# The cross-attention part of a perceiver block stepped by single groups, and eight wide products taken out of the delta-rule layers

## What is computed

```python
sa = attention(y, y, y, causal=True)
y = layernorm(y + sa, g1, beta1)
ca = attention(y, Z, Z, causal=False)      # Z: 257 rows of context for each sequence
y = layernorm(y + ca, g2, beta2)
h = jax.nn.relu(jnp.einsum('bsd,df->bsf', y, w1) + b1)     # DFF = 512
ff = jnp.einsum('bsf,fd->bsd', h, w2) + b2
y = layernorm(y + ff, g3, beta3)
```

## Time and profile before

| what | us |
|---|---|
| median of three runs | 762.5 |
| the profiled execution, whole time | 763.72 |
| its span, first to last instruction | 761.9 |
| first to last step of the cross part on VectorE | 8.6 to 111.7 |
| X in its new layout, VectorE goes on | 123.7 |
| the rest: two layers, routing, experts | 123.7 to 761.9 |
| mean granted TensorE clock | 0.853 |

### The profile page before, as it was taken

One profiled execution on the slowest core, in us unless ns is written; L12 is line 12 of the kernel. 1 busy time (PEld: TensorE's weight loads), 2 busy tenths in 40 slices (PEclk: granted clock), 3 DMA queues, 4 the chain that ended last, 5 costly groups with the idle time before them and its releaser, 6 DMA issues.

```text
span 761.9 us, 15678 instructions
## 1 busy us (share of the span) xinstructions
PE 625.3 (82%) x6640; PEld 427.1 (56%) x6640; DVE 461.8 (61%) x1124; ACT 256.4 (34%) x555; POOL 97.1 (13%) x140
## 2 busy tenths in 40 slices
PE   2777951786899999694997699978888799999995
PEld 1434641475688858464796678776444344444442
DVE  5846694978966354748828822475556855555552
ACT  1455510742421623642632034214323122222221
POOL 2535452300000001301100001010011000000000
PEclk9888985955599999897768658976899999999998
DMA  9994021000000000000000050000032163333321
GB/s 343 291 375 160 1 83 29 0 2 2 2 3 4 3 1 3 0 3 0 2 3 2 2 178 2 2 2 1 0 80 65 57 161 94 96 97 108 88 81 28
DMA packets 18981, 46.68 MB, mean 61 GB/s; under 512 B 3456, under 2 KB 8192, under 8 KB 18656
## 3 DMA queue, kind: packets, MB, share of 16 engines
q1 hardware_dynamic: 18368, 45.43, 19.3%
q10 hardware_dynamic: 544, 0.26, 0.1%
HBM read 43.32 MB, written 2.36 MB: 60 GB/s over the span
## 4 chain that ended last, share of the span: by engine, by line
PE 66%; DVE 22%; ACT 3%; DMA 3%; POOL 2%; issue 2%; SPq 1%; DVEq 0%; POOLq 0%
PE psum L753 7%; PE psum L748 7%; PE psum L758 7%; PE psum L685 5%; PE psum L594 5%; PE psum L560 3%; PE psum L711 3%; PE psum L714 3%; PE psum L674 3%; PE psum L621 3%; PE psum L667 2%; PE psum L720 2%; PE psum L571 2%; DVE yr L1287 2%; PE psum L464 2%; DVE pcT L1287 2%
## 5 line engine op out<-in xcount | busy, mean ns | idle before, releaser
L932 ACT ACTIVATE arena<-psum 128x512 f32<-128x512 f32 x68 | 40.6, 598 | 136.0 <-PE psum L748 122.9
L1363 DVE TENSOR_TENSOR arena<-psum,arena 128x512 f32<-128x512 f32 x64 | 44.2, 691 | 59.6 <-PE psum L753 57.8
L758 PE MATMUL psum<-arena,wed_sb 128*128 128x512 f32 x128 | 66.8, 604 | 0.0
L776 ACT ACTIVATE arena<-psum 128x512 f32<-128x512 f32 x56 | 33.3, 600 | 69.7 <-PE psum L560 41.0
L1368 DVE TENSOR_TENSOR arena<-arena 128x512 f32<-128x512 f32 x64 | 44.3, 692 | 14.0 <-PE psum L758 13.8
L560 PE MATMUL psum<-arena 32*64 32x128 f32 x1024 | 41.9, 327 | 6.6 <-ACT arena L776 2.8
L952 POOL TENSOR_TENSOR ve<-ss,eps_rms 128x4 f32<-128x4 f32 x16 | 3.7, 230 | 340.5 <-ACT yr L827 252.9
L560 PEld LDWEIGHTS psum<-arena 32*64 32x64 f32 x1024 | 36.8, 165 | 12.6 <-ACT arena L776 4.1
L753 PE MATMUL psum<-yT,weu_sb 128*128 128x512 f32 x68 | 36.3, 616 | 7.9 <-DVE arena L1363 7.9
L758 PEld LDWEIGHTS psum<-arena,wed_sb 128*128 128x128 f32 x128 | 24.6, 192 | 31.3 <-issue 22.7
L1314 DVE TENSOR_TENSOR arena<-psum,small 128x1024 f32<-128x1024 f32 x24 | 28.2, 1214 | 14.2 <-PE psum L667 14.2
(11 more groups left out here) (283 smaller groups left out, 1290.2 us busy)
## 6 DMA issues: line engine op xcount, KB each, us to landing
arena<-shares SPq DMA_DIRECT2D x64, 256.0 KB, 3.9
arena<-in_ctx_t SPq DMA_DIRECT2D x16, 514.0 KB, 8.9
arena<-in_ctx_z SPq DMA_DIRECT2D x16, 512.0 KB, 10.5
XA<-in_x SPq DMA_DIRECT2D x1, 1024.0 KB, 5.1
zlast<-in_ctx_last SPq DMA_DIRECT2D x4, 256.0 KB, 17.7
x_mid<-XA SPq DMA_DIRECT2D x4, 256.0 KB, 3.0
weg_sb<-in_we_gate SPq DMA_DIRECT2D x2, 512.0 KB, 6.5
weu_sb<-in_we_up SPq DMA_DIRECT2D x2, 512.0 KB, 7.5
```

The lines of the kernel that those rows point to most:

```text
L758: pe.matmul(x3, wed_sb[:, (p - 1) % (NPAIR + 1), :], act_a[pr], start=(p == 0), stop=False, skip_group_check=True).then_inc(x_down[pr], 1)
L776: return act.activation(out_, in_, ACT.Copy, scale=scale)
L932: act.activation(act_g[pr], banks[4 * pr + 2 * (n % 2)], ACT.Silu).then_inc(x_silu[pr], 1)
L1363: dve.tensor_tensor(act_gu[pr], banks[4 * pr + 1], act_g[pr], ALU.mult).then_inc(x_gu[pr], 1)
```

## The change

The cross part is no longer stepped by pairs but by single groups. Each group has a chain of its own up to its self attention (`BEFORE`) and one behind its cross attention (`AFTER`); the cross steps stay one chain for each pair. The letters a and b are `BEFORE` of the groups 0 and 1, c the cross steps of pair A, d and e `AFTER` of 0 and 1; v, w, x, y, z are the same for pair B. The transposes' removal from PSUM becomes a step of its own (`ev1`, `ev2`), and so does the last half of the last norm (`fin`, L1188). Counts for the waits come from a function instead of by hand; three semaphores are merged into others. A group's first transposes now land in its high bank, and the two banks of the feed-forward products are one low and one high bank of the group, so that `up` waits for the last use of the transposes' bank. GpSimd's bias for `XA` (L987) is one group at a time. SyncE's order of waits and copies stays. The engines' instructions are the same in number, but for the last hunk: the eight wide products in `lout` are removed.

```diff
-CROSS = ["st0", "nm0", "sas", "sap", "sar", "nm1", "c0", "c1", "c2", "c3", "c4", "c5", "cr0", "c6", "c7", "c8", "c9", "cr1",
-         "nm2", "up0", "up1", "dn", "nm3"]
-XTURNS = "AABAABABBABAAAAAABABABABAABABBAABBBABBBABABBBB"
+BEFORE = ["st0", "nm0", "sas", "sap", "sar", "nm1", "ev1"]
+AFTER = ["cr", "nm2", "ev2", "up", "dn", "nm3", "fin"]
+
+
+XTURNS = ("ababwvaavabvbaawbccvbvbcwcccwvvdcwxcxccdwwexdxxxydxdeyeyxdexxdzyezyyzyeezzzz")
...
+    chains = {}
+    for pr, (g0, g1, steps, h0, h1) in enumerate(("abcde", "vwxyz")):
+        for u, name in ((0, g0), (1, g1)):
+            chains[name] = iter([(kind, u, pr) for kind in BEFORE])
+        chains[steps] = iter([("c", n, pr) for n in range(NU * GT + 2)])
+        for u, name in ((0, h0), (1, h1)):
+            chains[name] = iter([(kind, u, pr) for kind in AFTER])
+    return [next(chains[turn]) for turn in XTURNS]
...
-                        pe.wait_ge(a_yT[pr], NU + (2 if n else 1))
+                        pe.wait_ge(a_yT[pr], count("yT", pr, "ev1", v))
...
+                low, high = banks[bank + u], banks[bank + 2 + u]
...
+                elif kind == "nm2":
+                    pe.wait_ge(a_norm[pr], count("norm", pr, kind, u))
+                    pe.wait_ge(at_exp[pr], count("exp", pr, "c", NT - NU + u))
+                    transposes(low, yn, g, a_tr[pr])
+                elif kind == "up":
                     pe.wait_ge(w_in, N_WEIGHT)
...
+                    if u == 0:
+                        pe.wait_ge(at_pT[pr], NT)
+                    for c in range(FFC):
+                        if c >= 2:
+                            pe.wait_ge(ff_h[pr], count("h", pr, kind, u) - FFC + c - 1)
+                        pe.matmul((high, low)[c % 2], w1_sb[:, c * P:(c + 1) * P], zT[g][:, :],
+                                  start=True, stop=True).then_inc(ff_up[pr], 1)
...
                     elif kind == "lout":
-                        if u == 0:
-                            dense(banks[bank + 2], 8)
                         pe.wait_ge(l_inv, pi + 1)
                         from_lanes(b1, pr, u).then_inc(l_omm[u], 1)
...
+                    if k == 2:
+                        pool.wait_ge(a_scaled[pr], count("scaled", pr, kind, u) - 2)
+                        pool.tensor_tensor(r[g], y[g], bc(rowv[:, B2:B2 + 1, :], [P, GT, D]),
+                                           ALU.add).then_inc(a_scaled[pr], 1)
+                        x_g = gcols(XA, g).rearrange("p (j c) -> p j c", j=GT)
+                        pool.wait_ge(a_vec[pr], count("var", pr, "nm0", u))
+                        pool.tensor_tensor(x_g, x_g, bc(rowv[:, BE3:BE3 + 1, :], [P, GT, D]),
+                                           ALU.add).then_inc(a_scaled[pr], 1)
...
+                elif kind == "fin":
+                    dve.wait_ge(a_rstd[pr], count("rstd", pr, "dn", u))
+                    dve.wait_ge(a_scaled[pr], count("scaled", pr, "nm2", u))
+                    st.reached(done[g])
```

More of the change, by code:

```diff
@@ L91, in cross_schedule, with count @@
 def cross_schedule():
-    streams = [iter(CROSS), iter(CROSS)]
-    return [(next(streams["AB".index(turn)]), "AB".index(turn)) for turn in XTURNS]
-XSTEPS = cross_schedule()
+    chains = {}
[6 more added lines that the diff above has]
+    return [next(chains[turn]) for turn in XTURNS]
+XSTEPS = cross_schedule()
+ONCE = lambda *kinds: {kind: 1 for kind in kinds}
+SIGNALS = {"var": ONCE("st0", "nm0", "sar", "cr", "dn"), "rstd": ONCE("st0", "sar", "cr", "dn"),
+           "norm": ONCE("nm1", "nm2"), "scaled": {"nm1": 1, "nm2": 3}, "tr": ONCE("nm0", "nm1", "nm2", "c"),
+           "yT": ONCE("nm0", "ev1", "ev2"), "scores": ONCE("sas", "c"), "max": ONCE("sas", "sap", "c"), "exp": ONCE("sas", "c"),
+           "pT": ONCE("c"), "out": ONCE("sap", "c"), "read": ONCE("cr"), "up": {"up": FFC},
+           "h": {"up": FFC}, "ff": ONCE("dn"), "done": ONCE("fin")}
+SIGNALLING = {"scores": (0, 8), "max": (0, 8), "exp": (0, 8), "tr": (1, 9), "pT": (1, 9), "out": (2, 10)}
+def count(name, pr, kind, u):
+    total = 0
+    for k, v, p in XSTEPS:
+        if p == pr and k in SIGNALS[name] and (k != "c" or v in range(*SIGNALLING[name])):
+            total += SIGNALS[name][k]
+        if (k, v, p) == (kind, u, pr):
+            break
+    return total
 def schedule():
@@ new lines, in _ @@
+                if kind == "c":
+                    n = u
+                    if n < NT:
+                        act.wait_ge(at_vec[pr], count("max", pr, kind, n))
+                        if pr == 1:
+                            act.wait_ge(ca_read[0], count("read", 0, "cr", n // GT))
+                        act.activation(pc[:, n, :], banks[bank + n % 2][:, 0:KEYS], ACT.Exp, bias=nmax[pr][:, n:n + 1],
+                                       accum_out=rsum[pr][:, n:n + 1]).then_inc(at_exp[pr], 1)
+                    if 1 <= n <= NT:
+                        act.wait_ge(a_tr[pr], count("tr", pr, kind, n))
+                        copy(pcT[:, n - 1, :], banks[bank + 2][:, 0:2 * P]).then_inc(at_pT[pr], 1)
+                    continue
@@ new lines, in _ @@
+                g = pr * NU + u
+                low, high = banks[bank + u], banks[bank + 2 + u]
+                if kind == "nm0":
+                    act.wait_ge(a_tr[pr], count("tr", pr, kind, u))
+                    copy(zT[g], high).then_inc(a_yT[pr], 1)
+                elif kind == "sas":
+                    act.wait_ge(at_vec[pr], count("max", pr, kind, u))
+                    act.activation(p1[g], s1[g], ACT.Exp, scale=SCALE_ATT).then_inc(at_exp[pr], 1)
+                elif kind in ("nm1", "nm2"):
+                    act.wait_ge(a_rstd[pr], count("rstd", pr, ("sar", "cr")[kind == "nm2"], u))
+                    for jj in range(GT):
+                        last = act.activation(yn[g][:, jj, :], r[g][:, jj, :], ACT.Identity, bias=shift[g][:, jj:jj + 1],
+                                              scale=rstd[g][:, jj:jj + 1])
+                    last.then_inc(a_norm[pr], 1)
+                elif kind == "ev1":
+                    act.wait_ge(a_tr[pr], count("tr", pr, "nm1", u))
+                    act.activation(zT[g], high, ACT.Identity, bias=gb1s[:, 1:2], scale=gb1s[:, 0:1]).then_inc(a_yT[pr], 1)
+                elif kind == "ev2":
+                    act.wait_ge(a_tr[pr], count("tr", pr, "nm2", u))
+                    act.activation(zT[g], low, ACT.Identity, bias=colv[:, C_G2 + 1:C_G2 + 2],
+                                   scale=colv[:, C_G2:C_G2 + 1]).then_inc(a_yT[pr], 1)
+                elif kind == "up":
+                    for c in range(FFC):
+                        act.wait_ge(ff_up[pr], count("up", pr, kind, u) - FFC + c + 1)
+                        act.activation(hT[g][:, c, :], (high, low)[c % 2], ACT.Relu,
+                                       bias=colv[:, C_B1 + c:C_B1 + c + 1]).then_inc(ff_h[pr], 1)
@@ new lines, in _ @@
+            for kind, u, pr in XSTEPS:
+                g = pr * NU + u
+                if kind in ("st0", "dn"):
+                    pool.wait_ge(a_vec[pr], count("var", pr, kind, u))
+                    rsqrt(st, g, mv[g][:, :, 1], GT, eps_ln, a_rstd[pr])
+                elif kind in ("sar", "cr"):
+                    pool.wait_ge(a_vec[pr], count("var", pr, kind, u))
+                    pool.tensor_tensor(shift[g][:, :], mv[g][:, :, 0], minus[:, :], ALU.mult)
+                    st.after(pool.tensor_tensor(ve[g][:, :], mv[g][:, :, 1], eps_ln[:, :], ALU.add))
+                    st.after(pool.tensor_tensor(rstd[g][:, :], ve[g][:, :], neg_half[:, :], ALU.pow))
+                    pool.tensor_tensor(shift[g][:, :], shift[g][:, :], rstd[g][:, :], ALU.mult).then_inc(a_rstd[pr], 1)
+                elif kind in ("nm1", "nm2"):
+                    k = int(kind[2])
+                    pool.wait_ge(a_norm[pr], count("norm", pr, kind, u))
+                    affine(g, (G1, G2)[k - 1], (BE1, BE2)[k - 1], st, a_scaled[pr])
+                    if k == 2:
[6 more added lines that the diff above has]
+                                           ALU.add).then_inc(a_scaled[pr], 1)
```

295 lines of the change are left out of this document (104 added, 191 removed).

## The result

| what | before, us | after, us | difference |
|---|---|---|---|
| median of five runs each | 762.5 | 766.4 | +3.9 |
| the profiled execution's span | 761.9 | 764.2 | +2.3 |
| last step of the cross part on VectorE ends | 111.7 | 116.3 | +4.6 |
| pair B's copies to memory issued, chain goes on | 110.7 | 116.7 | +6.0 |
| X in its new layout, VectorE goes on | 123.69 | 130.73 | +7.0 |

What follows compares the result with a forecast made beforehand. Bound: DMA up to 66 us, then the queues' order on PE and VectorE, a fixed bridge, then mostly PE. 762.5 us with 2.5 more for the cross part and 5.4 less for the wide products: 759.6, range 757 to 762.

Steps and rivals of the forecast that it cites:

- the wide one: Range of the whole time including the rivals: 754 to 767 us.
- Part 1: Cross part stepped by single groups: pair B's last write at 113.1 instead of 110.6 us, so 2.5 us more.
- The bounds: Cross part: -2.8 us if nothing collides in the new order, +6 if half clock falls on more feed-forward products.
- The collisions: Cross part: VectorE's two-input steps wait for GpSimd's wide operations; new order ends 1.4 us later, without them at 106.5.
- SyncE's queue: Cross part: group 1 and pair A's sixteen copies (6.3 us) go first, so pair B's last write leaves at 113.1, data there at 111.9.
- The new waits: Cross part: waits of `up`, `nm2`'s transposes and GpSimd's bias are on events already past, costing nothing.
- rival B: Half clock at L580 twice, 3.2 us each, and at `dn` of group 2, 3.7; 769.7 us, chance 0.12.
- the second and third place: Wide products there are on the chain for 1.83 and 1.73 us; removing them gains about 0.95 us each.
- Part 2: Removing the eight wide products at four places: 0 + 0.95 + 0.95 + 3.5, together 5.4 us gained.
- the first place: Wide products take 3.59 us on PE, but L580 still waits 0.57 us for the inverse: nothing gained.
- Rival C: Wide products were hidden anyway behind VectorE's chains, only 1 us gained; 764.0 us, chance 0.25.
- rival A: No collisions in the end of the cross part, which then gives 2.8 us; 754.3 us, chance 0.18.

Runs made afterwards that it cites:

- `a_wsplit`: Changed kernel with only w1 and w2 loaded ahead of the second ring loads, the other weights behind them: 764.6 us.
- `a_hold`: Changed kernel with eight wide products ahead of PE's wait before the second layer's values (L715): 761.1 us.
- the repairs: Narrow GpSimd operations and split weights, in the changed kernel also SyncE's copies in ending order: 757.4 us; old order without wide products: 755.4 us.
- `a_small`: Changed kernel with GpSimd's four wide operations behind the second norm on one tile of four, for timing only: 757.4 us.
- `b_small`: Kernel before with GpSimd's four wide operations behind the second norm on one tile of four, for timing only: 760.4 us.
- `a_dense8`: Changed kernel with the eight wide products put back, so only the new order of the cross part is left: 771.5 us.
- `a_sp`: Changed kernel with SyncE's copies of the cross part in the order in which the groups end (0, 2, 1, 3): 765.2 us.
- `a_narrow`: Changed kernel with every wide GpSimd operation in the norms issued as four narrow ones: 763.6 us.
- `b_all`: Kernel before without the eight wide products, with narrow GpSimd operations and the weights split: 755.4 us, ratio 0.989.
- `b_hold`: `b_all` with eight wide products ahead of PE's wait before pair A's values in the second layer: 748.8 us, ratio 0.981.
- `b_hold4`: `b_all` with four wide products ahead of PE's wait before pair A's values in the second layer: 750.0 us.

## Why the prediction was wrong

**The direction.** Forecast was 2.9 us faster, measured 3.9 slower. The sum had 2.5 - 5.4; the two profiles have 7.0 - 4.7. The 766.4 us lie outside the forecast's own range of 757 to 762 and just inside the wide one, which reached so far only by rivals. The step that failed is the issue of pair B's last write: forecast at 113.1, 2.5 us later than in the old order, it came at 116.7, 6.0 us later.

**Part 1, the end of the cross part: wrong by 4.5 us, and the mechanism of most of it was not in the working.** The two orders were written out with the waits that the code has. A pause behind no wait of the code, by all that the runs show for the instruction stream, could not come up. It enters as 3.4 us at 38 us, and pair B's last write comes 6.0 instead of 2.5 us later; the other 1.0 is the longer bridge, 4.66 instead of 3.78 for two writes at once and 6.42 instead of 6.26 behind. Without the pause (`a_wsplit`) X is in place 3.8 us later than before, of which 1.6 are the low clock at `dn` of group 2; this is near the forecast. How much of the median is the pause is less sure than how much of the trace: taking it away gave 3.2 us in the profile and 1.9 to 2.7 at the median. `a_hold`, with a pause of only 1.99 us, had X in place no earlier (130.60), since it lost 1.6 us to the clock in the same `dn`. At the median the new order costs 8.1 us against the old one, both without wide products (766.4 and 758.4); with the repairs it is 2.0 (757.4 and 755.4). The 6.1 between are pause, collisions, SyncE's order and the clock behind PE's wait together, and since they hide one another the runs give no share for each. The bounds, -2.8 to +6, did not hold 7.0: they came from the same two queues, and so could not contain what both left out.

**The collisions: right.** Forecast were 4.0 for L1132 of group 3, 5.0 for group 1 and 5.1 for group 0's last step; measured 4.23, 4.25 and 5.30. That they eat what the single groups give was right too: the cross part was to be 5.3 us shorter without them (-2.8 instead of 2.5; 5.7 in the expectation of `a_small`), and shrinking GpSimd's operations gave 6.6 in the end of X. That the old order had less to lose (1.3 in the expectation of `b_small`, 1.6 in the end of X) held as well, though it spends as much on them: its long ones stand beside other waits.

**SyncE's queue: right in kind.** It was forecast to be the limit by 1.2 us; it was by 0.4, since the pause had moved the data too. Turning its order gave 1.3 us at the median and 3.2 in the profile.

**The new waits at nothing: right. PE's wait: right in the changed kernel's profile by luck.** `up` waits for nothing at the transposes' bank. PE's long wait was placed at 91 us with 3.6 us by rival B and came at 95.3 with 3.88. It did not cost the clock in this profile, which stayed at 1.00 to 114 us. In those of `a_dense8`, `a_sp`, `a_hold`, `a_wsplit` and `a_narrow` it did, by 1.0 to 2.0 us in `dn` of group 2 behind it, so the mechanism of this part of rival B is real, at a quarter to a half of its price of 3.7. Its other part, a lost clock at the second and third place, did not come: L612 takes 3.90 and 3.92 us there.

**Part 2: the sum came out, its places did not.** L580's first product, counted from X in place, comes 0.0 us earlier at the first place (forecast 0; PE waits 4.10 us for the inverse instead of 0.57), 2.0 at the second, 1.6 at the third and 1.7 at the fourth, where 0.95, 1.9 and 5.4 had been forecast. The fourth place gave its 3.6, but as much was lost between the third and it, where more of the time was at half clock. The same four steps from 270 us behind X in place on (L656 to L560 before, L686 to L592 after) took 6.89 and 9.74 us, at a mean clock of 0.98 and 0.68, and the first half of L715 took 6.73 where L685 took 5.78:

```profile
393.86:400.75 6.89, 6.89 (x169) 6.26 (x168) 3.75 (x5) 3.92 (x8) 0.00 (x0) 0.98 0.01 2
399.22:408.96 9.74, 9.74 (x169) 8.68 (x169) 4.34 (x5) 4.08 (x8) 0.00 (x0) 0.68 0.01 2
```

The forecast had no term for the clock between the places. Between the fourth place and the gate's product (L729, 396.7 before, 392.6 after) 2.4 us came that I had nowhere, where one short stretch of half clock is missing, and 0.6 in the experts. So 4.7 near 5.4 is in part luck of the sum. (In its working, half of the third place's 1.73 is 0.87 and not 0.95; it changes nothing.) Rival C (hidden anyway) and rival A (no collisions) did not come true, but `a_narrow` comes near A's condition by hand.

**What the products do for the clock: only half of it was seen.** Rows 8 and 10 show that they do not raise a low clock, and that stands. Whether they hold a high one was left open, and only rival B had a price for it: products in a wait of PE hold a high clock, and at the fourth place, once the clock is high, four of them are worth 1.3 us. The Trainium skill (TensorE: Matmul & The Clock Gate, What you observe) says that under sustained matmul activity the products become almost twice as fast. In this case PE was full from 438.8 to 448.8 us in the changed kernel and stayed at 0.50, and the measurement decides. At two of the four places of the kernel before the clock was low already, and at the other two it stayed high without the products, so their removal was right there, and moving them would have been better.

## What to carry to other kernels

When two orders of the same work are written out from one trace, their difference is only as good as what both leave out; a pause behind no wait in the middle of a step, at full DMA engines, can be the instruction stream, and it went away here when loads that were not needed yet were issued later. Where VectorE has two inputs in SBUF beside a busy GpSimd, it waits for whole GpSimd instructions, so make these short. In this kernel filler products on PE paid in a wait that follows busy time at a high clock, and best with no more of them than the wait has room for; at a low clock they only cost (3.5 us at the fourth place). A new order also brings new waits of PE, and each is a place where a profile can show the clock high and the next execution low: several profiles are needed before it is called free.

## What the runs showed of the hardware that was not expected

- PE can stand still for 2.0 to 3.6 us between two instructions of one step while the DMA engines are full. It came in the profiles of the changed kernel, `a_dense8`, `a_sp`, `a_small`, `a_narrow` and `a_hold` (1.99 to 3.56 us), between the same two products of tile 5 each time and 2.4 to 2.7 us behind the start of an instruction packet, and in none in which products stood ahead of them or loads had been moved, nor in any of the old order.
- The same code of the cross part ends up to 3 us apart: X in place at 130.73 in the changed kernel, 133.63 in `a_dense8` and 130.60 in `a_hold`; 118.65 to 121.22 in `b_all` and the four versions built on it. In the new order the pause (3.37, 3.56, 1.99 us) and the clock behind PE's wait of 3.88 us (`dn` in 3.74, 5.76, 5.36 us) are most of it; in the old one it was not followed up.
- Four narrow GpSimd operations take 1.85 us where the wide one takes 1.27, and the kernel is 2.9 us faster by them.
- A wait of PE of 0.65 us is followed by half clock in `b_hold`; one of 0.98 us behind four wide products in `b_hold4` is not, nor one of 2.44 us without any products in the short execution of `a_dense8`, nor one of 3.88 us in the profile of the changed kernel. Length alone does not decide, and what does was not settled. That the short executions of the kernel before are made as that of `a_dense8` was not seen either, since none of them was profiled.
